# Cross keys and values projected during self-attention and kept in device memory, packed self scores, one query tile per cross step

## What is computed

```python
# self-attention: 32 heads of 16, ALiBi, causal
qkv = x @ w_qkv.T + b_qkv
scores = q @ k.T / sqrt(16) + slope[h] * (key_position - 255 .. 0)   # causal: -1e9 above the diagonal
x = layernorm(x + softmax(scores) @ v @ w_out.T + b_out)
# cross-attention: 32 query heads in 8 groups, 8 key/value heads of 128, rotary positions
q = rope(x @ wq);  k = rope(ctx @ wk);  v = ctx @ wv                  # ctx does not depend on x
x = layernorm(x + softmax(q @ k.T / sqrt(128) + mask) @ v @ wo)
# feed-forward: relu^2 (512 -> 1024 -> 512) plus a routed latent part
x = layernorm(x + ffn(x))
```

## Time and profile before

| | us |
|---|---|
| median of three runs | 1057.08 |
| the three runs | 1061.21, 1056.79, 1057.08 |
| span of the profiled execution, first to last instruction | 1065.3 |
| busy: TensorE matmul, weight load | 987.9 (93%), 825.1 (77%) |
| busy: VectorE, ScalarE, GpSimd | 765.2 (72%), 503.1 (47%), 437.0 (41%) |

### The profile page before, as it was taken

One profiled execution on the slowest core, in us unless ns is written; L12 is line 12 of the kernel. 1 busy time (PEld: TensorE's weight loads), 2 busy tenths in 40 slices (PEclk: granted clock), 3 DMA queues, 4 the chain that ended last, 5 costly groups with the idle time before them and its releaser, 6 DMA issues. The chain is left out here.

```text
span 1065.3 us, 17470 instructions
## 1 busy us (share of the span) xinstructions
PE 987.9 (93%) x4940; PEld 825.1 (77%) x4940; DVE 765.2 (72%) x2345; ACT 503.1 (47%) x1581; POOL 437.0 (41%) x367
## 2 busy tenths in 40 slices
PE   6997999999778999999999999999999999789996
PEld 5875999999556887887887887787778777578885
DVE  4445568888697787777877877777777788784646
ACT  4325669898335435445345435444444435441220
POOL 1762000000357556546546646637546455340101
PEclk9997579999899999999999999999999999999998
DMA  8032212222221102002002002002001002210001
GB/s 298 1 99 60 60 37 59 46 58 70 87 82 50 40 11 65 31 5 69 30 0 76 22 0 79 20 0 79 20 15 64 10 18 73 78 62 10 30 1 39
DMA packets 41372, 52.02 MB, mean 49 GB/s; under 512 B 5104, under 2 KB 21616, under 8 KB 41200
## 3 DMA queue, kind: packets, MB, share of 16 engines
q1 hardware_dynamic: 41008, 50.44, 15.6%
q0 software_dynamic: 320, 1.05, 0.3%
HBM read 40.98 MB, written 2.10 MB: 40 GB/s over the span
## 5 line engine op out<-in xcount | busy, mean ns | idle before, releaser
L1060 POOL TENSOR_TENSOR C_t<-C_t 128x512 f32<-128x512 f32 x80 | 104.5, 1310 | 153.2 <-DVE C_t L965 153.2
L817 ACT ACTIVATE C_prob<-C_prob,C_ntop 128x128 f32<-128x128 f32 x256 | 99.8, 391 | 87.9 <-DVE C_ntop L997 87.8
L34 PE MATMUL C_yb<-C_woh,C_oh 128*128 128x512 f32 x256 | 107.5, 420 | 17.4 <-POOL C_wol L1088 12.3
L774 ACT ACTIVATE C_qh<-C_t 128x512 fp32r<-128x512 f32 x64 | 40.5, 633 | 141.0 <-POOL C_t L1060 141.0
L1010 DVE TENSOR_TENSOR C_ol<-C_ov,C_oh 128x512 fp32r<-128x512 f32 x64 | 44.2, 691 | 85.8 <-ACT C_oh L792 85.8
L34 PE MATMUL C_pj<-xTh,wh 128*128 128x512 f32 x256 | 101.3, 396 | 3.7 <-DVE xTl L128 2.2
L492 ACT ACTIVATE B_prob<-B_prob,B_ntop 128x128 f32<-128x128 f32 x256 | 99.2, 392 | 8.5 <-DVE B_ntop L573 7.3
L34 PE MATMUL C_yb<-C_woh,C_ol 128*128 128x512 f32 x256 | 102.8, 402 | 0.0
L34 PE MATMUL C_yb<-C_wol,C_oh 128*128 128x512 f32 x256 | 102.6, 401 | 0.0
L34 PE MATMUL C_pj<-xTh,wl 128*128 128x512 f32 x256 | 100.8, 394 | 0.0
L34 PE MATMUL C_pj<-xTl,wh 128*128 128x512 f32 x256 | 100.6, 393 | 0.0
(11 more groups left out here) (219 smaller groups left out, 2867.1 us busy)
## 6 DMA issues: line engine op xcount, KB each, us to landing
stage<-wq_dram SPq DMA_DIRECT2D x32, 256.0 KB, 3.4
stage<-wo_dram SPq DMA_DIRECT2D x32, 256.0 KB, 3.1
qs<-q SPq DMA_DIRECT2D x16, 256.0 KB, 2.7
kd<-k SPq DMA_DIRECT2D x128, 32.0 KB, 2.0
stage<-wqkvT_dram SPq DMA_DIRECT2D x10, 256.0 KB, 5.9
x<-x_nat_dram SPq DMA_DIRECT2D x1, 2048.0 KB, 10.1
stage<-wk_dram SPq DMA_DIRECT2D x8, 256.0 KB, 3.2
stage<-ctxT_dram SPq DMA_DIRECT2D x8, 256.0 KB, 3.0
```

The lines of the kernel that those rows point to most:

```text
L34: mm = eng.matmul(out, stationary[i], moving[j], start=first and n == 0, stop=last and n == len(PASSES) - 1)
L817: last = eng.activation(e, e, ACT.Exp, bias=ntop[:, s % 2, h:h + 1], scale=1.0, accum_out=total[:, s % 2, h:h + 1])
L1060: eng.tensor_tensor(t1[:, j % 2, :], t1[:, j % 2, :], t2[:, j % 2, :], ALU.add).then_inc(s_sum, 1)
```

## The change

1. **Self scores.** Two heads of 16 are packed with their low parts, and a constant row that carries the bias, along the 128 rows of one matmul, and two heads' keys side by side in 256 columns. A step issues 2 matmuls of 256 columns in place of 3 of 512. VectorE adds one causal table in place of eight bias tables. For this, block A stores the split queries and keys in device memory (32 DMAs of 256 KB), and B loads each half batch by 8 DMAs.
2. **Cross keys and values.** The ctx pieces are split in A, while the value tiles are projected. In B each step carries half a projection (6 matmuls of 512 columns), 32 tiles in all: 16 of keys (rotated on VectorE, summed and split as in C) and 16 of values, whose product has the tokens on the rows, so that nothing is transposed. Results go to device memory; GpSimd does the low parts of all weight splits. Self-attention keeps one transpose bank in place of two, and `ot` and `yb` share one.
3. **Cross step.** No keys or values are projected. Each step rotates one query tile, n+4, and projects tile n+5. The rotation stands at the head of the step on VectorE. Keys and values of a group come by one 2 MB DMA into one of two buffers; `wo` and the transpose bank have two buffers each. All weight low parts are GpSimd's.
4. The loops of B and C are written out in full.

The diff, cut to its core:

```diff
@@ attend_self: tensor engine, step n = NG * b + G
-                    product(eng, sc[G % 2][:, :].rearrange("p (h s) -> p h s", h=HG), [qs[:, 2 * c + j, :] for j in range(2)],
-                            [kd[:, 2 * c + j, cols, :] for j in range(2)], True, True).then_inc(s_sc, 1)
+                    for i in range(2):
+                        j = 2 * (G % PAIR) + i
+                        mm = eng.matmul(sc[G % 2][:, 2 * S * i:2 * S * (i + 1)], heads.q[G // PAIR][:, j, :],
+                                        heads.k[G // PAIR][:, j, :], start=True, stop=True)
+                    mm.then_inc(s_sc, 1)
...
-                    wait(eng, s_phi, m - 1)
-                    wait(eng, s_plo, m - 1)
+                    wait(eng, s_phi, m)
+                    wait(eng, s_plo, m)
...
+                if 0 <= n - OFF < 2 * TILES:
+                    project((n - OFF) // 2, (n - OFF) % 2)
@@ attend_self: vector engine, behind plo and the output split
+                j = keys(n, 0)
+                if j is not None:
+                    eng.wait_ge(s_pj, 2 * j + 1)
+                    wait(eng, s_klo, j)
+                    eng.tensor_tensor(by_batch(t1[:, :]), by_batch(pj[0][:, :]), cos, ALU.mult).then_inc(s_cos, 1)
+                j = keys(n, 1)
+                if j is not None:
+                    eng.tensor_tensor(by_batch(t2[0:64, :]), by_batch(pj[0][64:128, :]), sin[0:64], ALU.mult)
+                    eng.tensor_tensor(by_batch(t2[64:128, :]), by_batch(pj[0][0:64, :]), sin[64:128],
+                                      ALU.mult).then_inc(s_sin, 1)
+                j = values(n, 0)
+                if j is not None:
+                    eng.wait_ge(s_vhi, j + 1)
+                    eng.tensor_tensor(v_out[:, :, 1, :], by_batch(pj[1][:, :]), v_out[:, :, 0, :].bitcast(F32),
+                                      ALU.subtract).then_inc(s_vlo, 1)
@@ attend_self: gpsimd
+                j = keys(n, 2)
...
+                    eng.tensor_tensor(k_out[:, :, 1, :], by_batch(t1[:, :]), k_out[:, :, 0, :].bitcast(F32),
+                                      ALU.subtract).then_inc(s_klo, 1)
+                for i in splits(n):
+                    hi, lo = target(i)
+                    ring.lo(eng, i, hi, lo)
+                j = keys(n, 1)
...
+                    eng.tensor_tensor(t1[:, :], t1[:, :], t2[:, :], ALU.add).then_inc(s_sum, 1)
@@ project_self: sync, behind the loads
+            for i in range(QK):
+                kind, m, h = order[i]
+                eng.wait_ge(s_vhi, i + 1)
+                eng.wait_ge(s_vlo, i + 1)
+                heads.store(eng, i, m, h, heads.tiles[i % heads.RING])
+            for n in range(EARLY, len(pieces)):
+                load_piece(eng, n)
+            heads.wait_stored(eng, QK // 2)
+            heads.load(eng, 0, 0)
+            for n in range(Ring.SLOTS):
+                eng.wait_ge(s_lo, max(j for j in range(len(pieces)) if j % RING == n) + 1)
+                selfring.load(eng, n, self_sources[n])
+            heads.load(eng, 0, 1)
...
+            for j in range(2):
+                heads.loaded(eng, 0, j)
@@ attend_cross: sync
+            load_kv(0)
             eng.dma_start(mask[:, :, :], mask_d).then_inc(s_const, 16)
@@ attend_cross: tensor engine
-                if projects(g, s):
-                    for j in STEPS[u]:
-                        project(H, g + s // 4, half, j)
+                if n + PRE + 1 < TILES:
+                    project(n + PRE + 1)
@@ attend_cross: vector engine
+            def step(n):
+                s = n % B
+                if live(n, 1):
                     eng.wait_ge(s_exp, n)
                     wait(eng, s_norm, n - 2)
-                    eng.reciprocal(rden[:, (s - 1) % 2, :], total[:, (s - 1) % 2, :]).then_inc(s_rden, 1)
-                if live(g, s, 2):
+                    eng.reciprocal(rden[:, (n - 1) % 2, :], total[:, (n - 1) % 2, :]).then_inc(s_rden, 1)
+                if n + PRE < TILES:
+                    rotate(n + PRE)
+                if live(n, 2):
                     eng.wait_ge(s_phi, n - 1)
...
-                if projects(g, s):
-                    for j in STEPS[u]:
-                        if j < V:
-                            rotate(H, j)
```

More of the change, by code:

```diff
@@ L285, in piece_hi @@
                     eng.wait_ge(s_acc, Q_DONE)
+                if pieces[n][0] == "ctx" and pieces[n][2] == 0:
+                    eng.wait_ge(heads.s_store[pieces[n][1]], 32 * (QK // heads.RING))
                 eng.activation(place(pieces[n], 0), slots[n % RING], ACT.Copy).then_inc(s_hi, 1)
@@ L369, in _ @@
                 if kind == "qk":
-                    t = q if m < C else k
-                    hi, lo = (t[:, 2 * (m % C) + j, h * HALF:(h + 1) * HALF] for j in range(2))
+                    hi, lo = (heads.tiles[i % heads.RING][:, j, :] for j in range(2))
                 else:
@@ L465, in _ @@
+            loop(eng, step)
             norm.roots(eng, 0)
@@ L705, in attend_cross @@
-        SPLITS = {2: [("wo", h) for h in range(Q)] + [("w", 0)], 3: [("w", 1), ("w", 2)],
-                  4: [("w", 3)], 5: [("w", K)], 6: [("w", V)]}
-        def splits(g, s):
-            return [x for x in SPLITS.get(s, ()) if not isinstance(g, int) or g < G - 1 or (g == G - 1 and x[0] == "wo")]
-        def slot(what):
-            kind, j = what
-            return (FIRST + (j if kind == "wo" else Q + j)) % RING
-        def next_pieces(g, s):
-            first = 2 * (B * g + s - NS + 4) if isinstance(g, int) else -1
+            for n in range(NS + 4):
+                step(n)
@@ L755, in _ @@
-            cycle(0)
-            with eng.Fori(1, G - 1) as g:
-                cycle(g)
-            cycle(G - 1, last=True)
-            eng.wait_ge(s_wlo, TILES * G)
-            for i in range(2):
-                eng.wait_ge(s_wolo[i], 2 * G)
+            for i in range(ring.SLOTS, len(sources)):
+                ring.load(eng, i, sources[i])
+                if i == 2 * Q - 1:
+                    load_kv(1)
+                if i >= 22 and (i - 22) % B == 0:
+                    load_kv((i - 22) // B + 2)
@@ L1104, in _ @@
-            for j in range(V):
-                first_lo(j)
-            for j in range(V):
-                tile_sum(0, j)
-                tile_lo(0, 0, j)
-                if j == 0:
+                if n + PRE < TILES:
+                    tile_sum(n + PRE)
+                    tile_lo(n + PRE)
+                if split(n) is not None:
+                    split_lo(split(n))
+                for i in next_pieces(n):
+                    if not weights.on_vector(i):
+                        weights.lo(eng, i)
```

799 lines of the change are left out of this document (399 added, 400 removed).

## The result

| | before | after |
|---|---|---|
| median of the runs, us | 1058.8 (1056.8 to 1061.2) | 1094.3 (1092.0 to 1096.9) |
| ratio, 95% interval | | 1.032 (1.028 to 1.036) |
| profiled span, us | 1065.3 | 1092.3 |
| forecast, us | | 1037.6 (1010 to 1064) |

The change makes the kernel 3.2% slower. The forecast was faster by 1.8%, and the result lies outside its range. Cross-attention did what was forecast. The loss is in blocks A and B and in the handover, which had been priced at +48 us together and took +98.5.

What follows compares the result with a forecast made beforehand. It took TensorE to bound block B and a VectorE-ScalarE chain to bound block C. 1065.3 + 48 (self-attention) + 0 (handover) - 67.5 (cross-attention) = 1045.8 us, less 8.2 gives 1037.6 us; range 1010 to 1064.

Steps and rivals of the forecast that it cites:

- The chain: Block C: a VectorE-ScalarE path with one rotation per step sets the pace, 8.5 us a step, between 8.3 and 8.75.
- The fast rival: Block C: GpSimd's new phase frees `C_ntop`, so TensorE sets 7.8 to 7.9 us a step; 1003 us, chance 0.12.
- 26.6 us a batch: Block B: TensorE's work for eight steps after the change, from 19.25 us, or 3.33 us a step.
- the rival: Block B: GpSimd's lock makes VectorE the bound, from five `B_ntop` caught per batch; up to 1072 us, chance 0.10.
- the 3.7: Block B: a self step over 3.7 us would show the forecast wrong; it expected 3.4.
- the last rival: Fourth rival, whole kernel: written-out code or DMA traffic costs, late half batches +28 us, 1066 us; chance 0.07.
- one transpose bank... room of about 2 us, so nothing: Block B: one bank in place of two delays nothing, as VectorE splits one step ahead of TensorE's transpose.
- The queries and keys are stored tile by tile, four tiles deep, hidden too.: Block A: the stores of split queries and keys cost no time, given a ring of four tiles.
- the eight ctx pieces: Block A: one ScalarE and one VectorE instruction per value tile, at most 1.3 us, hidden beside TensorE's 2.7 us.
- the last load: Block A to B: issued behind the last ctx piece, it starts B some 3 us later, at 92 instead of 89 us.
- the handover, 0: Block B to C: +2 us in B's tail and -2 us in C's prologue, together 0, between -5 and +5.
- I subtract it: Whole kernel: the profiled span's 8.2 us above the 1057.08 us median, taken off the 1045.8 us sum.

Runs made afterwards that it cites:

- e4: Changed kernel, with ScalarE copying the attention output (C_oh) ahead of the four exponentials in every step of block C: 1042.8 us, ratio 0.983.
- e10: Changed kernel, with most of GpSimd's low part of the rotated queries (C_ql) left out from the ninth query tile on: 1045.0 us, ratio 0.984.
- e1: Changed kernel, with block B's value-tile store issued one step earlier, ahead of the next half batch's eight loads: 1063.8 us, ratio 1.004.
- e3: Changed kernel, with block A's ctx loads issued between the query and key stores and the bias rows behind them: 1091.0 us, ratio 1.029.
- e9: e5, with the high parts of block A's queries and keys stored from ScalarE's queue, low parts still from SP's: 997.6 us.
- e5: Changed kernel with the edits of e1, e3, e4, plus earlier ctx copies and second heads load ahead of weight loads in block A: 996.1 us, ratio 0.933.
- e8: Changed kernel, with block C's fifth query projection, its rotation and copy moved behind step 0's scores, maximum and exponentials: 1094.4 us.
- e2: Changed kernel, with block C's mask loaded ahead of the first 2 MB of keys and values: 1095.6 us.

## Why the prediction failed

**Right: cross-attention.** The chain was read from the right rows and its new length worked out as 8.5; it measured 8.47, and 522.9 us against 524. e4 and e10 show both links of it. The fast rival named the right condition (`C_ntop` freed) and an end of 7.8 to 7.9 us; e10, where it is freed, has 7.53. Two readings on the way don't come out of the rows: a rotation adds 1.86 to 2.15 us (8.62 less 6.76, 10.77 less 8.62), and five rotations in four steps give 9.1 us a step where the group has 9.6, so the chain read in three steps did not account for the whole group. The forecast took its 8.5 from the step with one rotation, and neither reading entered it.

**Right: TensorE's batch in block B.** "26.6 us a batch" is 26.9 in e1 when nothing disturbs it. The single transpose bank costs nothing of its own, as forecast, and so do GpSimd's instructions there: e1 keeps both, and 14 of 64 `B_ntop` were stretched in the changed kernel, fewer than the five in eight from which the rival would have decided. The start was priced too high: e1's stage takes 209.9 us, 7 less than the forecast's 217.

**Failed: the price of the stores of keys and values in block B.** The self step, 240.9 us over 63, is 3.82 us, beyond the 3.7 that was named as the sign of being wrong. In the forecast the copies in device memory appear only in the last rival, as traffic of loads and a late half batch, "at most 2 us in each of 14". No half batch was late. What was late was the store of the value tile, and the step that failed is that no wait was looked for on it: one buffer, a store issued behind eight loads, and `pTh` behind the waiting copy on ScalarE. The step "one transpose bank... room of about 2 us, so nothing" was right of the bank alone; a stall of 3.5 us on ScalarE passes through it. Then the clock doubled the bill: 15.3 us of idle time became 31.0 us. The forecast allowed for a low clock at the start only, which was about right (back at 118.5 us, forecast 115).

**Failed: "The queries and keys are stored tile by tile, four tiles deep, hidden too."** The depth was compared with the time of a tile, not with what stands ahead in SP's queue. That wait was 8.25 us; e3 gives 4 to 6 back. 17.5 us of ScalarE's waits for stores are left in e3, and in e9 a second issuing queue does not shorten them. The last `A_val` is still 7.8 us later in e5 than in the kernel before (90.7 against 82.9).

**Failed: the eight ctx pieces, "hidden".** Each was priced as one instruction beside a tile of 2.7 us. The size was right (1.3 us by the forecast, 1.37 measured), but they form a loop with the tile: `A_val`, `vhl`, `cTh`, `cTl`, the next `A_val`, 3.19 us where TensorE has 2.72. `cTl` is 1.37 us long while GpSimd's `vhl` runs beside it; in e5, where ScalarE copies the piece one tile earlier, it is 0.68 in the median and the distance 2.72. That is the collision of VectorE and GpSimd again. An estimate from these rows: 3.19 less 0.69 is 2.5, so without it the loop would be under TensorE's pace. No run takes away the collision and keeps the order, so this share is not shown.

**Mis-sized: the last load, "some 3 us later".** From the last `A_val` to the first `B_ntop` it is 11.4 us where it was 6.1, 5.3 more. The load stood behind five weight loads that wait for ring slots; e5, without that order, has 4.7.

**Failed: the handover, 0.** It is +9.7. From the last `B_ntop` to block C's first copy it takes 22.9 us in place of 16.95: VectorE there has a rotation and a value split more (2.7 us), and TensorE two projection halves. From that copy to the first `C_ntop` it takes 40.2 in place of 36.4. One projection is gone, as counted (60 matmuls in place of 72), but the fifth one now needs the second half of the rows. In the kernel before the six projections and the rotations were done before that half was normalised, and the first maximum followed. Now VectorE has split the half at 403.9 us, waits for its projection, rotates for 2.1 us, and only then comes to the first maximum:

```profile
409.21 0.69 DVE L1058 TENSOR_TENSOR C_t<-C_pj,trig 128x512 f32<-128x512 f32 x1 [5.27 <-PE C_pj L34]
```

e8 shows that this work only moves, and that 5 us come back behind it; e2 shows that the mask was not the cause. The low clock stands for 23.9 us of the handover in place of 13.7; what part it has in the +9.7 was not tried, and so this cause stays open.

**Failed: "I subtract it", the 8.2 us.** The sum was made against a profiled span of 1065.3 us and moved down to a median of three runs. Twenty-seven further runs of the kernel before lie between 1056.4 and 1070.0 us, those below 1058.5 with a mean granted clock of 0.959 or 0.960, those above 1068 with 0.946 to 0.949. The profiled execution, about 1067 us as a whole, lies inside that range, with six of the 27 above it. The changed kernel's profile stood at its median. Of the 56.7 us of the miss 46.5 are in the stages; the other 10.2 are this step and the 2.0 us between a span and a whole time.

The bounds given for the parts (300 to 322, +-5, 8.3 to 8.75) add up to some 1012 to 1070 us and not to the 1018 to 1060 stated; and 300 us holds the 6 us of low clock though it is called warm. The result lies outside either range.

Of the rivals the fourth came closest in kind (traffic of the written copies, 1066 us) and was given 0.07. Its price had no clock in it and no part for block A.

## What to carry to other kernels

Write each engine's queue down in order before a store is called hidden: a store is only as early as the loads issued ahead of it, and the buffer's next writer waits for the landing. A stall of 3 us on an engine that is not the bound can cost TensorE twice, once as a wait and once as a low clock with it. Where VectorE and GpSimd have work at the same time, look at what the longer of two instructions adds to the loop, not only to the engine. And read off what the bottleneck engine needs without its chain: both kernels lost time in cross-attention to the place of one copy, 28 us before the change and 57 after it.

## What was not expected of the hardware

- Seven stops of TensorE, of 1.3 to 3.4 us, each came with a stretch at 1.2 GHz, five of 3.4 us, one of 6.8 and one of 10.3, though TensorE's row was full right behind them. Where the stops are gone (e1) the clock is 1.00 for 210 us.
- A GpSimd instruction of 1.28 us stretches a VectorE instruction on 128x4 numbers from 0.17 to 1.10 us. On a chain of 8.47 us, taking it away made the step 0.94 us shorter, which is all that TensorE left to win. The Trainium skill's rule of an exclusive lock held for a whole instruction ("SBUF — State Buffer", the section on the two separate sides) fits it, and e10 shows what it costs in this order of instructions: 49 us. In e4's order 30 steps keep the stretched instruction and lose nothing by it.
- 32 stores of 256 KB cost 1.2 us each to issue where they stand in one row on SP, 0.8 with waits and loads between them (e3), and 0.57 on SP and 0.59 on ScalarE where the two share them (e9); e9 and e5 differ by 1.5 us all the same.
